# A decoder layer on one core: the first batch's projections as plain f32 products of loaded tiles, in buffers of their own, with a new order of all engines

## The reference, cut to what matters

```python
x = x + attn(layernorm(x))        # one head of 128: q, k, v = xn @ w_q, w_k, w_v; softmax(q k^T / sqrt(128)) v @ w_o
xp = relu(layernorm(x) @ W.T + b) # cross attention to ctx, 512 rows of 256
yp = relu(ctx @ W.T + b)          # the context projection
x = x + softmax(mask(xp @ yp.T)) @ ctx
xq = act_quant(layernorm(x))      # ffn: ternary weights, 8-bit activations, inner 1024
x = x + act_quant(silu(xq @ gate.T) * (xq @ up.T)) @ down.T
```

## Time and profile before

| | |
|---|---|
| median of 3 executions | 382.35 us (381.49 to 382.92) |
| profiled execution | 382.19 us |
| its span, first to last instruction | 380.2 us |
| mean granted TensorE clock | 0.995 of full speed |
| TensorE, VectorE, ScalarE, GpSimd busy | 364.1, 319.8, 320.0, 294.2 us |

### The profile page before, as it was taken

One profiled execution on the slowest core, in us unless ns is written; L12 is line 12 of the kernel. 1 busy time (PEld: TensorE's weight loads), 2 busy tenths in 40 slices (PEclk: granted clock), 3 DMA queues, 4 the chain that ended last, 5 costly groups with the idle time before them and its releaser, 6 DMA issues.

```text
span 380.2 us, 7393 instructions
## 1 busy us (share of the span) xinstructions
PE 364.1 (96%) x2113; PEld 284.7 (75%) x2142; DVE 319.8 (84%) x921; ACT 320.0 (84%) x598; POOL 294.2 (77%) x425
## 2 busy tenths in 40 slices
...
GB/s 277 402 251 136 158 44 56 56 74 89 14 83 37 41 98 169 64 124 134 137 58 56 72 150 110 39 42 55 154 57 41 84 3 16 81 100 71 85 56 110
DMA packets 48167, 36.92 MB, mean 97 GB/s; under 512 B 39552, under 2 KB 41216, under 8 KB 47744
## 3 DMA queue, kind: packets, MB, share of 16 engines
...
...
## 4 chain that ended last, share of the span: by engine, by line
PE 79%; ACT 7%; DVE 5%; DMA 4%; issue 3%; POOL 1%; ACTq 0%; DVEq 0%; POOLq 0%; SPq 0%
PE b_bank L1047 9%; PE b_bank L1049 9%; PE b_bank L1048 9%; PE d_bank L1251 7%; PE a_bank L1047 6%; PE a_bank L1049 6%; PE a_bank L1048 6%; PE g_bank L1235 5%; PE u_bank L1235 5%; PE b_bank L1163 3%; PE a_bank L1093 3%; DMA a_xT_raw<-in_x_t 2%; PE e_bank L1047 1%; PE e_bank L1049 1%; PE e_bank L1048 1%
## 5 line engine op out<-in xcount | busy, mean ns | idle before, releaser
L674 POOL TENSOR_TENSOR c_work<-c_work 128x512 f32<-128x512 f32 x48 | 61.8, 1290 | 18.1 <-DVE c_work L1491 16.1
L716 POOL TENSOR_SCALAR c_work<-c_work,h_q 128x1024 f32<-128x1024 f32 x31 | 34.9, 1125 | 11.5 <-DVE h_q L1511 11.5
L1504 DVE TENSOR_REDUCE h_max<-c_work 128x1 f32<-128x1024 f32 x32 | 38.8, 1213 | 4.2 <-POOL c_work L674 3.6
L935 ACT ACTIVATE c_work<-g_bank,c_tanh_scale 128x512 f32<-128x512 f32 x52 | 36.0, 692 | 6.4 <-PE g_bank L1235 4.9
L1047 PE MATMUL b_bank<-ctx_hi,b_pT_hi 128*128 128x256 f32 x128 | 38.6, 302 | 0.0
L1491 DVE SCALAR_TENSOR_TENSOR c_work<-c_work,g_bank 128x512 f32<-128x512 f32 x52 | 35.3, 679 | 2.1 <-ACT c_work L935 1.8
L1049 PE MATMUL b_bank<-ctx_hi,b_pT_lo 128*128 128x256 f32 x128 | 36.1, 282 | 0.0
L1048 PE MATMUL b_bank<-ctx_lo,b_pT_hi 128*128 128x256 f32 x128 | 36.1, 282 | 0.0
L1251 PE MATMUL d_bank<-downT,c_half 128*128 128x256 bf16 x256 | 33.3, 273 | 1.5 <-ACT a_xT_raw L962 0.9
L945 ACT ACTIVATE c_half<-c_work 128x1024 bf16<-128x1024 f32 x28 | 29.7, 1066 | 4.1 <-POOL c_work L716 4.1
L1235 PE MATMUL g_bank<-gateT,xqT 128*128 128x512 bf16 x98 | 30.5, 381 | 1.5 <-ACT xqT L908 0.5
...
## 6 DMA issues: line engine op xcount, KB each, us to landing
...
r_bc<-r_rows SPq DMA_DIRECT2D x7, 256.0 KB, 3.8
...
c_work<-in_w_up SPq DMA_DIRECT2D x1, 1024.0 KB, 10.2
```

What stands on the lines that cost most here:

```text
L674: pool.tensor_tensor(h[:, t % 2, half * HALF:(half + 1) * HALF], th[:, j % 2, :], up[:, j % 2, :], ALU.mult).then_inc(hs, 1)
L716: pool.tensor_scalar(h[:, t % 2, :], h[:, t % 2, :], h_q[:, t:t + 1], ROUND if n < LAST else ROUND_F16, ALU.mult, ALU.add).then_inc(h_roun ...
L935: act.activation(th[:, j % 2, :], gu_bank("g", j, n), ACT.Tanh, scale=c_tanh_scale[:, j // 2:j // 2 + 1]).then_inc(tanhs, 1)
L1504: dve.tensor_reduce(h_max[:, one], h[:, t % 2, :], AX.X, ALU.max, apply_absolute_value=True).then_inc(h_maxes, 1)
```

## The change

- **Own buffers.** The first batch's x^T goes into `xT_first`, a view of `c_xn`, and its ctx^T into `ctxT_first`, a view of `b_xn`; both are first written by later steps. All of these loads are issued by SP (`W.t0`, `W.t1`, `W.c0`, `W.c1`), none by ScalarE. `load_xT(1)` and `load_ctxT(1)` wait for nothing.
- **Plain products.** Q, K, V of batch 0 are two plain f32 matmuls each, of the centred weights as they lie in `wqkv_raw` and `xT_first` (`project_first`). YP0 and YP1 of batch 0 are two plain f32 matmuls each, of `W_raw` and `ctxT_first`. The steps `W.cT0`, `W.cT1`, `A.xT0/0`, `A.xT1/0` go from ScalarE's and VectorE's lists. The split centred weights and the split W are first read by batch 1.
- **r row** in bank b1 instead of b0; it waits for the centring, and the weight totals (`F.total`) wait for its copy.
- **Norm of B, batch 0** waits for `e_filled` 2, since it writes into `b_xn`.
- **A new order** on all five engines for the whole run, and new bank tables for the front.

The diff, with the order lists cut to the stretch that the prediction speaks of (old, then new) and renamings and removed semaphores left out:

```diff
-FRONT_BANKS = ["e", "b0", "a0", "a1", "g", "u", "d", "a0", "a1", "e", "g", "u", "d"]
+FRONT_BANKS = ["a0", "a1", "g", "e", "b0"]
+FRONT_TURN = ["u", "d", "a0", "a1", "e", "g", "u", "d", "a0", "a1", "g"]
+A_FRONT = """Q/0 K/0 V/0 VT/0 S0/0 YP0/0 S1/0 YP1/0 S2/0 S3/0 Q/1 P0/0 K/1 P1/0 V/1 P2/0 P3/0 YP0/1 VT/1 S0/1
...
 PE_ORDER
-    W.colsum/0 E.YP0/0 E.YP1/0 A.Q/0 A.K/0 A.V/0 W.r/0 A.VT/0 A.S0/0 A.S1/0 A.S2/0 A.S3/0 A.P0/0 A.P1/0 A.Q/1
-    A.K/1 A.P2/0 A.P3/0 A.V/1 E.YP0/1 A.VT/1 A.S0/1 A.S1/1 A.H/0 A.S2/1 A.P0/1 E.YP1/1 A.Y0/0 A.Y1/0 A.S3/1
-    A.P1/1 F.total/0 A.P2/1 E.YP0/2 A.P3/1 E.YP1/2 A.H/1 B.XT0/0 B.XT1/0 A.Y0/1 A.Y1/1 B.XP0/0 B.XP1/0 A.Q/2
...
-    B.P3/7 C.g5/6 B.O2/7 C.u5/6 B.O3/7 C.g6/6 C.xT0/7 C.g7/6 C.DN0/6 C.u6/6 C.u7/6 C.g0/7 C.DN1/6
...
+    W.colsum/0 A.Q/0 A.K/0 W.r/0 A.V/0 E.YP0/0 A.VT/0 A.S0/0 A.S1/0 A.S2/0 A.S3/0 A.Q/1 A.P0/0 A.K/1 E.YP1/0
+    E.YP0/1 A.P1/0 A.V/1 A.P2/0 A.P3/0 E.YP1/1 A.VT/1 A.S0/1 A.S1/1 A.H/0 A.S2/1 A.P0/1 E.YP0/2 A.Y0/0 A.Y1/0
+    A.S3/1 A.P1/1 E.YP1/2 A.P2/1 F.total/0 A.P3/1 A.H/1 B.XT0/0 B.XT1/0 A.Y0/1 A.Y1/1 B.XP0/0 B.XP1/0 A.Q/2
...
+    B.XP0/1 B.XP1/1 A.Y0/2 A.Y1/2 C.u0/0 A.Q/3 C.u1/0 B.S0/1
...
+    B.O1/7 C.g5/6 C.u6/6 C.DN0/6 B.P3/7 B.O2/7 C.u7/6 C.g6/6 C.xT0/7 C.g7/6 B.O3/7 C.DN1/6
...
 ACT_ORDER
-    W.cT0/0 A.xT0/0 A.xT1/0 W.cT1/0 W.hi/0 W.qkv/0 E.YP0/0 W.rh/0 A.Q/0 F.sum0/0 E.YP1/0 F.sum1/0 W.r/0 A.K/0
+    A.xT0/1 A.xT1/1 W.rh/0 W.qkv/0 A.Q/0 W.hi/0 A.K/0 W.r/0 F.sum0/0 F.sum1/0 A.VT/0 E.ctxT/1 E.YP0/0 W.wo/0
+    A.exp0/0 A.exp1/0 A.Q/1 B.mask/0 A.P0/0 A.exp2/0 A.K/1 A.exp3/0 F.sum2/0 E.YP1/0 F.sum3/0 A.P1/0 E.YP0/1
+    B.ctx/0 A.P2/0 A.P3/0 E.ctxT/2 A.VT/1 E.YP1/1 F.sum4/0 A.exp0/1 F.sum5/0 A.H/0 A.P0/1 A.exp1/1 A.exp2/1
+    E.YP0/2 A.xT0/2 A.xT1/2 A.P1/1 A.exp3/1 A.P2/1 E.ctxT/3 A.P3/1 E.YP1/2 B.norm0/0 B.norm1/0 A.H/1 B.XT0/0
 DVE_ORDER
-    W.cT0/0 A.xT0/0 A.xT1/0 W.cT1/0 W.lo/0 W.centre/0 A.bn0/0 A.bn1/0 A.ag0/0 W.split/0 A.ag1/0 A.bn0/1 A.bn1/1
+    A.bn0/0 A.ag0/0 A.bn1/0 A.ag1/0 W.centre/0 W.rs0/0 W.rl/0 W.split/0 W.rs1/0 W.lo/0 A.Q/0 A.K/0 A.V/0 A.bn0/1
 POOL_ORDER
...
+    C.rs1/0 C.xq0/0 C.scales0/0 C.xq1/0 B.XP0/1 B.XP1/1 C.scales1/0
...
 SP_ORDER
-    W.c0/0 W.qkv/0 W.c1/0 W.W/0 W.x0/0 W.x1/0 S.x/1 W.bias/0 W.o/0 W.hm/0 F.gate/0 F.up/0 F.down/0 S.ctx/0
+    W.x0/0 W.qkv/0 W.x1/0 W.t1/0 W.bias/0 W.t0/0 S.xT/1 W.c1/0 W.W/0 W.c0/0 F.gate/0 W.o/0 W.hm/0 S.x/1 S.ctxT/1
+    F.up/0 S.ctx/0 S.mask/0 F.down/0 S.xT/2
...
+        xT_first = c_xn[:, :, :].rearrange("p t d -> p (t d)").rearrange("p (c s) -> p c s", c=DC)
+        ctxT_first = b_xn[:, :, :].rearrange("p t d -> p (t d)").rearrange("p (c s) -> p c s", c=DC)
...
-            for c in range(DC):
-                act.dma_start(a_xT_raw[:, c, :], x_t[:, 0, c, :]).then_inc(xT0_loaded[c], 16)
...
+            def project_first(dst, step):
+                w = "QKV".index(step)
+                if step == "Q":
+                    pe.wait_ge(qkv_centred, 1)
+                for c in range(DC):
+                    if step == "Q":
+                        pe.wait_ge(xT0_loaded[c], 16)
+                    mm = pe.matmul(dst[:, :], wqkv_raw[:, c, w, :], xT_first[:, c, :], start=c == 0, stop=c == DC - 1)
+                return mm
...
-                if step in ("V", "Q", "K"):
+                if step in ("V", "Q", "K") and n == 0:
+                    mm = project_first(dst, step)
+                elif step in ("V", "Q", "K"):
...
             def e_step(c, n):
+                if n == 0 and c == 0:
+                    pe.wait_ge(W_loaded, 16)
...
                 for k in range(DC):
+                    if n == 0:
+                        if c == 0:
+                            pe.wait_ge(ctxT0_loaded[k], 16)
+                        mm = pe.matmul(dst[:, :], W_raw[:, k * D + c * P:k * D + (c + 1) * P], ctxT_first[:, k, :], start=k == 0, stop=k == DC - 1)
+                        continue
...
                 elif name == "r":
                     pe.wait_ge(r0_spread, 1)
-                    pe.wait_ge(e_relus, 2)
+                    pe.wait_ge(qkv_centred, 1)
```

More of the change, by code:

```diff
@@ L29 @@
 ROUND_F16 = ROUND + F16_BITS
-A_FRONT = """YP0/0 YP1/0 Q/0 K/0 V/0 VT/0 S0/0 S1/0 S2/0 S3/0 P0/0 P1/0 Q/1 K/1 P2/0 P3/0 V/1 YP0/1 VT/1 S0/1
+A_FRONT = """Q/0 K/0 V/0 VT/0 S0/0 YP0/0 S1/0 YP1/0 S2/0 S3/0 Q/1 P0/0 K/1 P1/0 V/1 P2/0 P3/0 YP0/1 VT/1 S0/1
     S1/1 H/0 S2/1 YP1/1 P0/1 Y0/0 Y1/0"""
@@ L44, in a_tables @@
     later = A_NEXT.split() + [f"{step}/{n}" for n in range(2, 8) for step in A_STEPS.split()]
-    cycle = FRONT_BANKS[2:]
-    use = list(zip(front, FRONT_BANKS[:2] + [cycle[i % len(cycle)] for i in range(len(front) - 2)]))
+    use = list(zip(front, itertools.chain(FRONT_BANKS, itertools.cycle(FRONT_TURN))))
     turn = itertools.cycle(NEXT_BANKS)
@@ L89 @@
-    C.u5/1 C.g5/1 B.O2/2 A.Q/4 A.K/4 B.O3/2 B.XT0/3 A.V/4 C.u6/1 C.g6/1 B.XT1/3 C.DN0/1 C.u7/1 E.YP0/5 C.g7/1
-    A.VT/4 A.S0/4 B.XP0/3 C.DN1/1 A.S1/4 B.XP1/3 C.u0/2 A.P0/4 A.S2/4 E.YP1/5 C.DN2/1 A.P1/4 B.S0/3 B.S1/3
-    C.g0/2 A.S3/4 B.P0/3 B.S2/3 C.g1/2 C.DN3/1 B.P1/3 B.O0/3 A.P2/4 C.g2/2 A.P3/4 C.u1/2 B.S3/3 C.g3/2 A.H/4
-    C.u2/2 B.P2/3 B.O1/3 C.u3/2 A.Y0/4 A.Y1/4 C.g4/2 C.u4/2 B.P3/3 B.O2/3 C.u5/2 C.g5/2 A.Q/5 B.O3/3 C.g6/2
-    A.K/5 A.V/5 C.DN0/2 C.u6/2 A.VT/5 A.S0/5 C.u7/2 B.XT0/4 B.XT1/4 E.YP0/6 A.S1/5 C.g7/2 B.XP0/4 B.XP1/4 A.P0/5
@@ L99 @@
-    B.S3/5 B.P2/5 C.u4/4 A.H/6 C.g4/4 B.O1/5 B.P3/5 E.YP0/7 A.Y0/6 B.O2/5 A.Y1/6 A.Q/7 A.K/7 B.O3/5 C.g5/4 A.V/7
-    C.u5/4 B.XT0/6 B.XT1/6 A.VT/7 C.u6/4 A.S0/7 C.g6/4 B.XP0/6 C.u7/4 B.XP1/6 A.S1/7 A.P0/7 C.u0/5 C.g7/4 A.S2/7
-    C.DN0/4 A.P1/7 A.S3/7 C.g0/5 B.S0/6 A.P2/7 B.S1/6 C.g1/5 B.P0/6 C.u1/5 A.P3/7 E.YP1/7 B.S2/6 B.P1/6 A.H/7
-    C.u2/5 C.g2/5 B.O0/6 A.Y0/7 B.S3/6 B.P2/6 A.Y1/7 C.g3/5 C.u3/5 B.O1/6 B.P3/6 C.u4/5 C.g4/5 B.O2/6 B.O3/6
-    C.g5/5 C.u5/5 C.DN1/4 B.XT0/7 B.XT1/7 C.u6/5 C.g6/5 C.DN2/4 C.u7/5 B.XP0/7 C.g7/5 C.DN3/4 B.XP1/7 C.DN0/5
```

329 lines of the change are left out of this document (157 added, 172 removed).

## The result

The changed kernel takes 382.90 us (median of 20 executions, 381.42 to 386.94), the kernel before in the same job 381.69 us (median of 20, 380.63 to 382.92). The ratio is 1.0035, 95% interval 1.0018 to 1.0051: 0.35% slower, a difference inside the half per cent that the prediction called no change, but on the other side from the forecast of 379.4. The profiled execution took 383.67 us, with a span of 381.6 and a mean granted clock of 0.991.

What follows compares the result with a forecast made beforehand. TensorE's own work was taken to bound the long middle, so gains had to come from front or tail. 382.19 - 3.0 (front) + 0.3 (middle) = 379.5, rounded to 379.4 us; range 378.2 to 380.8.

Steps and rivals of the forecast that it cites:

- Start of Q/0: Front: batch 0's Q starts at about 10.35 us instead of 12.90, 2.55 earlier, at most 2.66.
- Data: Loads at the start: batch 0's and batch 1's inputs land with enough cover; costed at nothing.
- Plain products: Batch 0's front: a plain f32 product takes 1.73 us, 0.36 more than a split one; five products.
- TensorE's own sum: Front up to XP1/0: 43.2 us of work from 10.35 ends at 53.6, 4.5 us earlier if TensorE never waits.
- ScalarE sets what is had, Q/2 at 55.1: Front: ScalarE's list and waits put Q/2 at 55.1 us, 3.0 us earlier; bounds 1.0 and 4.5.
- the first rival: Front: ScalarE's waits stay 2.3 us and a 1.7 us low-clock stretch returns; 380.9 us, chance 0.21.
- The roundings that go: ScalarE and VectorE before 9 us: dropping four roundings and four rests gains nothing more.
- The dense middle: Interleaved middle: work kept, holes possible between XP1/n and S0/n; +0.3 us, bounds 0 and 3.
- The tail: Tail: five steps, 2.7 us, move ahead of O3/7; net nothing, from -1 to +1.5 us.
- front half won: The name of the first rival: front gains only part, total 380.9 us, chance 0.21.

Runs made afterwards that it cites:

- e7: Changed kernel with fourteen filling matmuls ahead of H/1 and ten ahead of g2/7; 381.19 us, ratio 0.9991 to the kernel before.
- e12: e7 with roundings of 1/std and centred weights ahead of batch 1's x^T on ScalarE, 1/std's second spreading ahead of the weight split on VectorE; 380.35 us, ratio 0.9965.
- e2: Changed kernel with fourteen filling matmuls ahead of g2/7, inside its 1.74 us wait; 382.24 us, ratio 1.0017 to the kernel before.
- e10: Changed kernel with four of six weight sums on ScalarE taken over 64 of 1024 columns, leaving out computation; 381.98 us, ratio 0.9997 to the kernel before.
- e1: Changed kernel with fourteen filling matmuls into an unused bank ahead of H/1, inside its wait; 381.23 us, ratio 0.9996 to the kernel before.
- e3: Changed kernel with YP1/2 moved behind P3/1 on TensorE and ctx^T/3's rounding behind P3/1's on ScalarE; 381.98 us, ratio 1.0019 to the kernel before.
- e5: Changed kernel with S3/1 three steps earlier in its own bank, P1/1 to P3/1 and YP1/2 behind it; 383.65 us, ratio 1.0049 to the kernel before.

## Why the prediction was wrong, point by point

The profiled 382.19 us against which all sums are made lie 0.16 us below the median shown, not above it; this changes no sum.

1. **Start of Q/0.** Predicted 10.35, measured 10.30. Right, though other profiles of the same front show 8.8 to 10.3, by the length of the warm-up, which I took as fixed. The gain at Q/0 "cannot exceed" 2.66 us only if it is; in e7 it is 4.09 (12.90 less 8.81).
2. **Data.** The transfers needed by batch 0 cost nothing. But "batch 1's x^T lands near 8 ... which have that much cover too" was wrong: I asked only when TensorE reads it. ScalarE could round it from 9.05 us here, from 8.8 to 9.8 in the other profiles of this front, and in the new order it heads ScalarE's list, so 1/std waits behind it. In the profile of the changed kernel, where Q/0 starts late, this costs little: from Q/0 to VT/0 it is 7.72 us there and 7.43 in e12, and VT/0 came 0.2 us later than my sum had it (17.8). Where Q/0 starts early, the broadcast waits 1.3 to 2.0 us and the clock may fall behind that wait (e2, e10), a place for a low clock that neither the forecast nor a rival had. e12 starts VT/0 1.17 us earlier than e7. (The 0.90 us for ScalarE's two issues stand in the trace of before, not in the earlier trace rows.)
3. **Plain products.** 1.73 predicted, 1.72 measured.
4. **TensorE's own sum.** Sound as arithmetic, but it compares an old front that has a low-clock stretch with a new one that has none. The old kernel has the stretch only in most executions, and its price from VT/0 to XT0/0 is 1.11 us and not 1.7, since waits behind it take part up.
5. **ScalarE sets what is had, Q/2 at 55.1.** This is the step that failed. Q/2 came at 58.25, 3.15 late. In the prediction's own terms: it put TensorE's work from Q/0 to Q/2 at 43.2 us, the waits at 1.5 (55.1 less 53.6) and the low clock at nothing. Measured are 47.95 us with 3.63 idle (the row above) and 1.55 lost to the clock in H/1, which leaves 42.8 for the work. So the work was right, the waits are 2.1 us more than allowed, and the low clock is 1.55 more.

   The low clock: I had priced the wait at H/1 (1.8 us, measured 2.06) and had then written the clock off for S0 to S3 alone; the first rival had it, but for the wrong place. e1 shows this part by experiment.

   The waits: the text itself names 0.8 ahead of P1/0 and 1.8 at H/1 (less what TensorE is itself late), and then allows 1.5 for all of them together; 0.51 and 2.06 came, with 0.63 ahead of Y0/1 that the old front has too and 0.29 ahead of YP0/1. The count of ScalarE's list was wrong as well. Four weight sums stood ahead of VT/0 in the old order, not two, and the new order moves none ahead but two behind it (four of six against two). By the terms that are given the list would hold 35.65 + 2.3 - 2.1 - 1.0 = 34.9 us of work, and its start at 18.4 leads to 53.3 without a hole; the 56.2 that stand there do not follow from them. Measured, ScalarE is busy for 38.09 of the 41.73 us from VT/0 to Q/2's rounding. By e10 its excess costs about 1 us in the front, but it does not make the wait at H/1.

   What makes that wait: TensorE reaches S3/1 at 41.60, because it must now make YP1/0 and the plain YP0/0 behind Q/0, and P3/1's transposes at 45.19. From there to H/1 a rounding on ScalarE and a rest on VectorE take 2.68 us, and nothing of TensorE's stands between. The old front has the same latency (46.32 to some 49.0) with YP1/2 as cover in it. Other entries on both lists lengthen it: in the changed kernel ScalarE's rounding is done and VectorE is free within 0.1 us of each other, e3 moved only the entry on ScalarE and gained nothing, and in e5, where both are out of the way, it is 2.16 us (45.32 to 47.48). But e5 waits 1.25 us ahead of P3/1 and 1.37 ahead of Y0/1, so an order in which TensorE does not wait for this chain at all was not found, and whether there is one stays open. At full clock VT/0 is 2.06 us ahead (20.34 and 18.28), and the stretch from there to XT0/0 is 2.12 us longer (32.71 against 30.59), about what YP1/0 takes there with the wait behind it (24.46 to 26.62 in the changed kernel): nothing is left.
6. **The roundings that go.** Worth nothing, as said.
7. **The dense middle.** +0.3 predicted; from XT0/0 to xT0/7 the new order takes 301.9 to 302.5 us in the table and the old 302.1 to 302.5: equal. In e3 and e5, whose fronts end differently, it is 303.6 and 303.9. A new wait stands ahead of VT/4, for the broadcast of its 1/std by DMA (0.51 us here, 1.24 in e3); it is the one price of the new middle that I found in the profiles.
8. **The tail.** "Nothing, from -1 to +1.5"; measured +1.75 (24.69 less 22.94), of which 0.4 is the order (23.34 at full clock) and 1.3 the second low-clock stretch behind the gathered wait of 1.74 us. I summed work between steps and never asked how waits are divided: from xT1/7 to 371 us the old order has 0.20, 0.25, 0.92, 0.24 and 0.92 us, the new one 1.74, 0.19, 0.48 and 0.33.

By the table the profiled execution of after stands 0.19 us behind before at XT0/0, wins 0.62 in the middle and loses 1.75 in the tail, 1.32 in all: the forecast's 3.0 us shrink to nothing in the front, and in these two profiles the tail decides the sign. Over all executions it is not the tail's low clock alone: the eleven of 20 with about one low stretch have a median span of 380.5 us, and the kernel before had some 379.7 (381.69 less the 2.0 around the span). How these eleven divide among the broadcast, H/1 and the tail no profile shows. The rival "front half won" came nearest in mechanism (a low-clock stretch returns), not in time (380.9).
